# Six local attention and MLP layers on one core: another order of every engine's stages, and of the sync engine's stores, loads and moves

## The reference, cut to what matters

```python
for i in range(6):
    x = attn_layer(shift_tokens(x), Wqkv[i], q_scale[i], k_scale[i], Wo[i]) + x
    x = ffn_layer(shift_tokens(x), ln_g[i], ln_b[i], W1[i], b1[i], W2[i], b2[i]) + x

def attn_layer(x, Wqkv, qs, ksc, Wo):       # 16 heads of 64
    q, k, v = jnp.split(x @ Wqkv, 3, -1)    # (3 x 1024 wide)
    q = l2norm(q) * qs;  k = l2norm(k) * ksc
    q = q * cos * scale + rotate_half(q) * sin * scale
    k = k * cos / scale + rotate_half(k) * sin / scale
    out = local_attention(q, k, v)          # windows of 32, looking one window back, softmax
    return out @ Wo

def ffn_layer(x, g, bln, W1, b1, W2, b2):
    xn = (x - mean) / jnp.sqrt(var + 1e-05) * g + bln
    a, gate = jnp.split(xn @ W1 + b1, 2, -1)        # 341 wide each
    return a * jax.nn.gelu(gate) @ W2 + b2
```

## Time and profile before

| | us |
|---|---|
| time, median of 3 runs (range) | 3554.08 (3550.71 to 3567.42) |
| the profiled execution's own time | 3559.78 |
| its span, first to last instruction | 3557.9 |
| PE busy | 3278.1 (92% of the span) |
| DVE busy | 2950.5 (83%) |
| POOL busy | 2629.0 (74%) |
| ACT busy | 2266.0 (64%) |
| mean granted TensorE clock | 0.982 of full speed |

### The profile page before, as it was taken

How to read it: one execution, slowest core, us unless ns; L and a number is a source line. 1 busy time by engine, 2 the same in 40 slices (tenths; PEclk the granted TensorE clock), 3 DMA queues, 4 the chain that set the end, 5 groups by cost and what they waited for, 6 DMA issues and landing times.

```text
span 3557.9 us, 129156 instructions
## 1 busy us (share of the span) xinstructions
PE 3278.1 (92%) x55618; PEld 1918.6 (54%) x55618; DVE 2950.5 (83%) x3295; ACT 2266.0 (64%) x4196; POOL 2629.0 (74%) x1408
## 2 busy tenths in 40 slices
PE   8978999999999999999999999999999999987996
PEld 4545555555555555555555555555555555543554
DVE  7869888888888888888888888888888888854787
ACT  6865566666565666656565666666665656656895
POOL 1139888787888878887888887787878888852666
PEclk9989999999999999999999999999999999998998
DMA  2003333433333433333333334333333333340000
GB/s 91 2 1 91 114 103 109 121 111 107 109 109 108 126 104 114 103 108 115 109 109 115 109 102 122 109 115 109 101 120 112 109 114 109 97 125 19 2 11 16
DMA packets 229182, 335.95 MB, mean 94 GB/s; under 512 B 39047, under 2 KB 151045, under 8 KB 228229
## 3 DMA queue, kind: packets, MB, share of 16 engines
q1 hardware_dynamic: 228612, 327.68, 30.0%
HBM read 124.14 MB, written 102.76 MB: 64 GB/s over the span
## 4 chain that ended last, share of the span: by engine, by line
PE 74%; issue 10%; DVE 7%; ACT 5%; POOL 2%; DMA 1%; SPq 0%; DVEq 0%; POOLq 0%; ACTq 0%
PE psum L721 28%; PE psum L789 9%; PE psum L775 8%; PE psum L816 7%; PE psum L748 5%; PE psum L731 5%; PE psum L827 3%; DVE f_times_sin L1016 2%; ACT f_squares L885 1%; PE psum L798 1%; ACT x_expo L1467 1%; PE psum L806 1%; ACT x_expo L383 1%; DVE f_gelu L1088 1%; PE psum L1324 1%
## 5 line engine op out<-in xcount | busy, mean ns | idle before, releaser
L1149 POOL TENSOR_TENSOR f_rotated<-f_rotated,f_rnorm 128x1024 f32<-128x1024 f32 x384 | 722.7, 1903 | 534.1 <-ACT f_rnorm L896 533.8
L721 PE MATMUL psum<-w_qkv,f_xs 128*128 128x512 f32 x2304 | 1093.4, 608 | 21.3 <-DVE f_times_sin L1016 11.3
L1141 POOL TENSOR_TENSOR f_rotated<-f_times_cos,f_times_sin 128x1024 f32<-128x1024 f32 x384 | 908.3, 2366 | 9.2 <-DVE f_times_sin L1016 9.2
L903 ACT COPY f_qkT<-psum 128x1024 f32<-128x1024 f32 x384 | 369.7, 1014 | 472.5 <-PE psum L731 472.4
L721 PEld LDWEIGHTS psum<-w_qkv,f_xs 128*128 128x128 f32 x2304 | 419.3, 192 | 465.8 <-issue 434.8
L1015 DVE TENSOR_TENSOR f_times_cos<-psum,rot 128x1024 f32<-128x1024 f32 x384 | 464.0, 1208 | 111.1 <-ACT f_squares L885 110.3
L885 ACT ACTIVATE f_squares<-psum 128x1024 f32<-128x1024 f32 x384 | 393.5, 1025 | 208.2 <-PE psum L721 184.2
L1016 DVE TENSOR_TENSOR f_times_sin<-psum,rot 128x1024 f32<-128x1024 f32 x384 | 465.4, 1212 | 0.0
L1023 DVE TENSOR_REDUCE f_sumsq<-f_squares 128x16 f32<-128x1024 f32 x384 | 463.8, 1208 | 0.0
L775 PE MATMUL psum<-f_probsT,f_v 64*64 64x32 f32 (+1 forms) x6144 | 314.0, 229 | 94.9 <-issue 94.8
L775 PEld LDWEIGHTS psum<-f_probsT,f_v 64*64 64x64 f32 x6144 | 267.1, 137 | 242.7 <-issue 242.7
(11 more groups left out here) (175 smaller groups left out, 5016.9 us busy)
## 6 DMA issues: line engine op xcount, KB each, us to landing
f_v_moved<-f_v SPq DMA_DIRECT2D x768, 128.0 KB
turned_blocks<-w_qkv SPq DMA_DIRECT2D x192, 512.0 KB, 3.0
f_probsT<-turned_blocks SPq DMA_DIRECT2D x768, 128.0 KB
w_qkv<-in_l_wqkv SPq DMA_DIRECT2D x18, 512.0 KB, 4.0
w_o<-in_l_wo SPq DMA_DIRECT2D x6, 512.0 KB, 4.4
w_qkv<-in_ctxT SPq DMA_DIRECT2D x1, 2048.0 KB, 9.3
out<-x_f_result SPq DMA_DIRECT2D x8, 256.0 KB, 2.2
w<-in_l_w SPq DMA_DIRECT2D x6, 341.0 KB
```

The costliest lines, as they stand in the source:

```text
L721: mm = pe.matmul(pairs[i][:, j * BANK:(j + 1) * BANK], xs[g % 2][:, u % GB, :], w_qkv[:, part * INNER + j * BANK:part * INNER + (j + 1) * ...
L903: act.copy(qkT[u % 2][:, part].rearrange("p t n -> p (t n)"), pair(("qT", "kT")[part], u)).then_inc(copied[part], 1)
L1141: pool.tensor_tensor(rotated[u % 2][:, part].rearrange("p h (s d) -> p s h d", s=2), halves(times_cos[part][:, :]), halves(times_sin[part] ...
L1149: pool.tensor_tensor(rt, rt, rnorm[u % 2][:, part * H:(part + 1) * H].unsqueeze(2).broadcast_to([P, H, HD]), ALU.mult).then_inc(normalised ...
```

## The change

No instruction of the stack is added or removed, no shape changes. What changes is the order of stages within a step, and the lag of some: v is projected at step - 3 (before step - 2) and copied at step - 3; `lower` runs at step - 2 (before step - 4), `exponentials` and `row_sums` at step - 3 (before step - 4); `mlp_root`, `mlp_affine`, `mlp_shift` and `prepare` one step nearer to what they wait for. The thirds run 0, 1 on PE, ACT and DVE. On SP the stages are now called by step: placement, loads, store, moves. The group stages keep their lags on PE, so the four kinds of steps stay.

```diff
             LAST = 14
-            ROTATING = (("q", 0, 1), ("mix", 6, 1), ("up2", 13, GB), ("v", 2, 1), ("variance", 9, GB), ("k", 0, 1), ("down", 13, GB),
-                        ("scores", 2, 1), ("up1", 12, GB), ("out", 6, GB), ("up0", 12, GB), ("kT", 1, 1), ("qT", 1, 1), ("mean", 8,
+            ROTATING = (("q", 0, 1), ("mix", 6, 1), ("up2", 13, GB), ("v", 3, 1), ("k", 0, 1), ("variance", 9, GB), ("scores", 2, 1),
+                        ("out", 6, GB), ("down", 13, GB), ("up0", 12, GB), ("up1", 12, GB), ("kT", 1, 1), ("qT", 1, 1), ("mean", 8,
                         GB))
...
             def sp(sp):
-                for u in range(UNITS + 3):
-                    layer, into = (u + 3) // NB, (u + 3) % NB
-                    if layer < DEPTH and into == 0:
-                        load_qk(sp, layer, 0)
-                    if u >= 3:
-                        place_probs(sp, u - 3)
-                    if layer < DEPTH and into == 0:
-                        load_qk(sp, layer, 1)
-                    if u < UNITS:
-                        place_v(sp, u)
-                    layer, into = (u + 1) // NB, (u + 1) % NB
-                    if 0 < layer < DEPTH and into == 0:
+                for step in range(UNITS + LAST):
+                    place_probs(step - 5, sp)
+                    layer, into = step // NB, step % NB
+                    if 0 < layer < DEPTH and into == 5:
+                        load_out(sp, layer)
+                    if 0 < layer < DEPTH and into == 12:
+                        load_mlp(sp, layer)
+                    if 0 < layer < DEPTH and into == 2:
                         load_v(sp, layer)
-                    if 0 < layer < DEPTH and into == 4:
-                        load_out(sp, layer)
-                    if 0 < layer < DEPTH and into == 11:
-                        load_mlp(sp, layer)
+                    if layer < DEPTH - 1 and into == NB - 1:
+                        load_qk(sp, layer + 1, 0)
+                        load_qk(sp, layer + 1, 1)
+                    store_probs(step - 4, sp)
+                    place_v(step - 3, sp)
...
                     project(step, 0)
                     mix(step - 6)
                     mlp_up(step - 13, 2)
-                    project(step - 2, 2)
+                    project(step - 3, 2)
+                    project(step, 1)
                     mlp_variance(step - 9)
-                    project(step, 1)
+                    scores(step - 2)
+                    project_out(step - 6)
                     mlp_down(step - 13)
-                    scores(step - 2)
+                    mlp_up(step - 12, 0)
                     mlp_up(step - 12, 1)
-                    project_out(step - 6)
-                    mlp_up(step - 12, 0)
                     transpose_qk(step - 1, 1)
                     transpose_qk(step - 1, 0)
                     mlp_mean(step - 8)
...
-                for step in range(-2, UNITS + LAST):
+                for step in range(-1, UNITS + LAST):
+                    prepare(step + 1)
                     mlp_square(step - 9)
-                    mlp_root(step - 10)
                     square(step, 0)
                     copy_mix(step - 6)
                     mlp_gelu(step - 13, 2)
                     reciprocal_norms(step - 1)
-                    mlp_shift(step - 8)
-                    exponentials(step - 4)
+                    exponentials(step - 3)
+                    copy_v(step - 3)
                     square(step, 1)
-                    copy_v(step - 2)
-                    prepare(step + 2)
-                    mlp_affine(step - 11)
+                    mlp_gelu(step - 12, 0)
+                    mlp_affine(step - 10)
                     mlp_log(step - 9)
                     mlp_gelu(step - 12, 1)
-                    mlp_gelu(step - 12, 0)
                     copy_qk(step - 1, 1)
+                    mlp_root(step - 9)
+                    mlp_shift(step - 7)
                     copy_qk(step - 1, 0)
...
+                    turn_probs(step - 5)
                     products(step, 0)
-                    turn_probs(step - 5)
+                    sum_squares(step, 0)
                     mlp_hidden(step - 13, 2)
-                    row_sums(step - 4)
+                    row_sums(step - 3)
                     products(step, 1)
+                    mask_scores(step - 2)
+                    mlp_hidden(step - 12, 0)
                     add_down(step - 13)
-                    mask_scores(step - 2)
                     mlp_hidden(step - 12, 1)
-                    mlp_hidden(step - 12, 0)
-                    sum_squares(step, 0)
-                    mlp_centre(step - 8)
-                    add_out(step - 6)
-                    row_maxima(step - 2)
                     sum_squares(step, 1)
                     clamp_norms(step)
+                    add_out(step - 6)
+                    mlp_centre(step - 8)
+                    row_maxima(step - 2)
...
                 for step in range(UNITS + LAST):
+                    normalise_probs(step - 4)
+                    normalise(step - 1, 0)
+                    normalise(step - 1, 1)
                     mlp_scale(step - 10)
-                    lower(step - 4)
-                    normalise(step - 1, 1)
-                    normalise(step - 1, 0)
+                    rotate(step, 1)
                     rotate(step, 0)
-                    normalise_probs(step - 4)
-                    rotate(step, 1)
+                    lower(step - 2)
```

More of the change, by code:

```diff
@@ L647, in load_mlp, with place_v @@
                     sp.dma_start(v_ln[:, i:i + 1], dram[s][layer].rearrange("(p a) -> p a", a=1)).then_inc(mlp_loaded, 16)
-            def place_v(sp, u):
+            @each(UNITS)
+            def place_v(u, sp):
                 src, dst = v[u % 4], v_moved[u % 4]
@@ L660, in place_v, with store_probs @@
                     sp.dma_start(dst[HD * half:HD * half + HD, 1, :], src[WIN:3 * WIN, half, :]).then_inc(v_placed, 16)
-            def place_probs(sp, u):
+            @each(UNITS)
+            def store_probs(u, sp):
                 sp.wait_ge(probs_turned, u + 1)
@@ L668, in place_probs @@
                 sp.dma_start(turned_blocks[u % 2], w_qkv[:, 3 * INNER:]).then_inc(probs_stored, 16)
+            @each(UNITS)
+            def place_probs(u, sp):
                 sp.wait_ge(probs_stored, 16 * (u + 1))
```

## The result

The changed kernel takes 3464.25 us (median of 4, 3458.59 to 3476.63), the kernel before 3557.39 in the same session: ratio 0.974, 95% interval 0.970 to 0.978. It is faster by 93 us. The time is 31 us (0.9%) above the forecast of 3433, and inside the range. In a later session the same comparison gave 0.971 (0.969 to 0.974).

The account below looks back on a forecast made before the run. PE sets the pace, busy 2612.28 of 2753.29 us. Terms -76.8 - 46.3 - 5.0 - 9.1 - 11.3 + 27 = -121.5 took the profiled 3559.8 to 3438.3, median 3433 us; range for 8 in 10: 3390 to 3500.

Parts of the forecast that it names:

- Mix, -76.8: PE's waits before mix go, 76.8 us: earlier turning leaves 11.0 us for a store-to-mix chain taken as 8.5.
- 10.4: Upper end, in us, of the store-to-mix chain if the placement lands only behind all the moves.
- Mean, -46.3: PE's waits before the mean, 43.1 us plus 3.2 at layer borders, go with third 0 before third 1.
- Clock, -11.3: PE's busy time falls by 11.3 us if the lower clock follows the long waits and goes with them.
- New waits, +27: PE's k transposes wait 0.4 us for POOL each bare step, plus 0.2 for close misses: 27 us.
- q's 9.1 at the step's start: PE's q waits 0.2 us each for the bare step's k products; these waits go, 9.1 us.
- The loop through POOL: Products, rotations and sums on DVE and POOL take 11.8 us against a 10.8 us bare step; expected to fit by 0.2.
- rival 1: The DVE and POOL loop is not absorbed: waits of 2.0 us a group, not 0.6; 3496 us, chance 0.13.
- Rival 2: Slower: moves delay store and placement, so mix waits in up and down steps; 3640 us at chain 14, chance 0.05.
- Layer borders, -5.0: At layer borders k's weight load goes out some 5 us earlier, so q's waits of 5.0 us go.
- Fill, 0 +- 10: Filling and emptying the pipeline cost nothing, bounds 10 us either way.

Follow-up runs that it names:

- b_turn: The kernel before with one edit: on DVE the turning of the probabilities stands ahead of products(step, 0); 3542 us, ratio 0.991.
- b_thirds: The kernel before with one edit: thirds 0 and 1 of the MLP trade places on PE, ACT and DVE; 3526 us, ratio 0.986.
- a_start: The changed kernel with q and k weight loads ahead of the placement and start_layer ahead of the previous layer's last row maxima; 3454 us, ratio 0.971.
- a_turn: The changed kernel with the turning of the probabilities put back one place on DVE, behind products(step, 0); 3573 us, ratio 1.005.
- a_border_norm: The changed kernel with q and k weight loads ahead of the placement and POOL normalising k before q; 3462 us, ratio 0.970.
- b_both: The kernel before with two edits, thirds 0 and 1 swapped and the turning ahead of products(step, 0); 3489 us, ratio 0.977.
- b_dve: b_both with the changed kernel's order of DVE instructions, at the old distances in steps; 3563 us, ratio 0.998.

## Why the prediction was right, and where the 31 us are

In the profiled executions the gain is 83.2 us (93 in the medians) where 121.5 were forecast. (The profiled execution of the changed kernel is the slowest of its four, so 38.3 are missing here and fewer in the medians.) The 38.3 are 17.6 in the 45 groups and 20.8 outside them, less rounding.

- *Mix, -76.8*: gone, as forecast, from 11.0 us of room against a chain of 8.3 (taken: 8.5; moves cost 8.3 - 7.4 = 0.9 and not up to 3.0). Spare 2.7; the forecast had 3.6 without the moves and 2.5 with its 8.5. In the median of 44 such chains the placement's last packet ends 7.7 us after the store's issue (6.7 before), and the moves' last one 5.6 us after it. The Trainium skill (DMA: Bandwidth & Descriptors, Queues, rings and completion order) says that on each DMA engine descriptors are consumed in ring order and that a completion is written only after every earlier write. The trace agrees so far that the placement always ends behind the moves. It doesn't bear out the 10.4 that I had read from the rule: the placement's first packets mostly start before the moves' last, and the placement ends only 1.0 us later than before. But b_turn shows that I had not priced what the earlier turning displaces: q's products, 1.1 us later in the up step, and the scores behind them (53 us). In the full order this shrinks to 9.9 us, by something that the forecast didn't know it needed: that its sum came out inside the layers is in this part luck.
- *Mean, -46.3*: right, in the change and alone (b_thirds: -49).
- *Clock, -11.3*: right. PE's busy time fell by 12.5 us; it is 57.77 us in a group at a granted clock of 1.00, and the clock was lower only in the first group (0.94) and at two borders (0.97).
- *New waits, +27*: 22.1 at the transposes, 0.41 in each bare step as worked out, and 9.9 at the scores (not named): 32. q's 9.1 at the step's start went; 5.3 at three borders came.
- *The loop through POOL*: absorbed, rival 1 fell; the transposes of the up steps do not wait. Rival 2 fell with the chain at 8.3.
- *Layer borders, -5.0*: **this step failed.** I said that k's loads go out "some 5 us earlier" and that the wait goes. They stand behind a placement, and q, which as before starts 5.1 us after the last load, waits 2.1 us. PE's waits at the borders are 10.7 and 5.3 us, where 5.0 were to go. Behind the loads start_layer, which I had not priced (0.9 us before), takes 4.3 us beside POOL's instructions. Borders cost 5 x 4 = 20 us over the usual group, which covers the 17.6. a_start takes 14 of them back.
- *Fill, 0 +- 10*: **mis-sized.** It cost 20.1 up to the first project_out. Two windows each, first of the kernel before, then of the changed one:

```profile
15.00:30.00 15.00, 11.36 (x89) 6.59 (x87) 9.48 (x11) 8.41 (x27) 1.67 (x2) 1.00 0.77 262
250.00:380.00 130.00, 107.10 (x1996) 64.98 (x1998) 120.33 (x117) 70.62 (x90) 114.92 (x57) 0.96 0.29 87
```
```profile
15.00:30.00 15.00, 12.21 (x69) 7.46 (x68) 7.71 (x8) 7.82 (x23) 1.27 (x1) 0.80 0.78 267
250.00:380.00 130.00, 100.09 (x1654) 62.48 (x1655) 104.95 (x106) 61.57 (x79) 101.76 (x50) 0.85 0.22 67
```
6.8 us of it is not the change's: between 15 and 30 us, in code that is the same, the granted clock was 0.80 (some of it at 1.2 instead of 2.4 GHz). PE ran 1.0 us late before the clock fell at 24 us; by 36 us, shortly before it rose again, the delay was nearly 6 us, and all that follows starts later. b_thirds, whose code there is also untouched, had 0.80 too, and a_turn and a_border_norm, of the new order, had 1.00. The other 13.3 belong to the fill: in the new order DVE and POOL have gaps there, and the fill took 125 to 131 us against 118. With k normalised first the fill took 122 to 123, so this gives back 2 to 9; the rest (the rotations' order, the distances in steps) was not tried. How much of the fill the lower clock took is not shown either (0.85 and 0.90 between 250 and 380 us in two executions of the same kernel, fills of 131 and 125 us).

What takes the scores' wait from 54.7 to 9.9 us, beyond the two edits of b_both, can be followed in the traces. The stretch on DVE from the end of the bare step's k products to the end of the up step's q products takes 7.1 us before (medians of 40 steps), 8.2 in b_turn and b_both, longer by the turning (1.1), and 7.4 in the changed kernel, where the first sum of squares has moved ahead of the k products and out of the stretch. In b_dve it is out of it too, and the stretch takes 9.3: the clamp in it takes 2.41 us, where the changed kernel's takes 0.18. So DVE's order is worth 1.1 us in the up step as long as the clamp stays short. Which of POOL's order, the shorter distances and v's step keeps it short there stays open: no run tried them apart.

## What to carry to other kernels

Put first in a step what waits for nothing of that step: one place back on an in-order engine cost 3%. The neighbour's length (2.3 us) would have fitted in the spare of 2.7; with the neighbour's wait it came to 5. When something moves forward, price what it pushes back, down to who needs that bank. Give borders and the fill terms of their own; here they held the error, but for 6.8 us of a lower clock early on, while the steady group came out at 58.4 us against 58.5.

## What the runs showed of the hardware

A small DVE instruction can last as long as POOL's beside it: the clamp (128x32, in and out in SBUF) 0.18 us at its shortest and 2.41 beside a rotation, the products of start_layer (128x64, two SBUF inputs) 0.21 and 1.92. DVE's products and reductions (1.2 us, from PSUM or with one SBUF input) kept their length beside POOL.

The changed kernel's trace shows when. All 192 clamps start while a POOL instruction runs. The 56 that start in its last 0.2 us take 0.18 to 0.24; the other 136 end 0.03 to 0.04 us after it does. In b_dve 54 of the 192 outlast the POOL instruction that they start beside and end with the next, such as this one of 3.55 us:

```profile
906.03 3.55 DVE L1031 TENSOR_SCALAR f_sumsq<-f_sumsq 128x32 f32<-128x32 f32 x1
905.33 2.35 POOL L1141 TENSOR_TENSOR f_rotated<-f_times_cos,f_times_sin 128x1024 f32<-128x1024 f32 x1
907.64 1.89 POOL L1127 TENSOR_TENSOR f_probs<-f_probs,f_negmax 128x1024 f32<-128x1024 f32 x1
```

The Trainium skill (SBUF — State Buffer, Who interferes with whom) names this contention: DVE and GpSimd share a pair of ports as an exclusive lock, a DVE instruction contends with two SBUF inputs or in a two-port mode, which a tensor_scalar can enter, and whoever issues first has the pair for its whole instruction. The traces agree that the small instruction is blocked and not slowed in proportion; the rows of b_dve show in addition that it can stay blocked through the POOL instruction behind. The changed kernel's DVE loses 92 us to its clamps that the kernel before did not. Moving the clamp to where POOL stands still is the next thing to try.
